# Softmax rows transposed by 32x32 squares on VectorE and through DRAM, with the next image's convolution placed inside attention

## What is computed

```
hdn = relu(w1[m] @ perceive(x)[m] + b1)      # 32 models, 9*16 shifted channels -> 64
x   = x + w2[m] @ hdn + b2                   # 64 -> 16 channels of each model
theta, phi, g = (W_t x + b_t), (W_p x + b_p), (W_g x + b_g)     # 512 -> 128
attn = softmax(theta^T phi)                  # 1024 x 1024 per image
out  = batchnorm(W_w (attn g) + b_w) + x     # 128 -> 512
```

## Time and profile before

| | before |
|---|---|
| median of 3 runs | 1656.85 us |
| the profiled execution's own time | 1657.71 us |
| its span, first to last instruction | 1655.7 us |
| TensorE / VectorE / ScalarE / GpSimd busy | 98% / 43% / 47% / 15% |
| mean granted TensorE clock | 0.992 |
| DMA queue q1, share of 16 engines | 42.0%, 210.65 MB |

### The profile page before, as it was taken

How to read it: one execution, slowest core, us unless ns; L and a number is a source line. 1 busy time by engine, 2 the same in 40 slices (tenths; PEclk the granted TensorE clock), 3 DMA queues, 4 the chain that set the end, 5 groups by cost and what they waited for, 6 DMA issues and landing times.

```text
span 1655.7 us, 26446 instructions
## 1 busy us (share of the span) xinstructions
PE 1617.6 (98%) x9476; PEld 952.3 (58%) x9476; DVE 706.1 (43%) x1200; ACT 774.1 (47%) x1349; POOL 243.3 (15%) x134
## 2 busy tenths in 40 slices
PE   5899999999999999999999999999999999999998
PEld 1276482845738466483754838457384664837557
DVE  0154262543626345262542625335263452625436
ACT  1444454544455454454544545444554544545444
...
GB/s 283 152 157 52 219 81 98 193 38 250 57 125 159 51 250 51 163 126 83 206 51 229 72 107 182 38 263 51 131 158 40 249 51 186 102 88 200 51 0 51
DMA packets 82238, 210.83 MB, mean 127 GB/s; under 512 B 7728, under 2 KB 42544, under 8 KB 82224
## 3 DMA queue, kind: packets, MB, share of 16 engines
q1 hardware_dynamic: 82224, 210.65, 42.0%
...
...
## 4 chain that ended last, share of the span: by engine, by line
PE 89%; issue 3%; DVE 3%; ACT 2%; DMA 2%; SPq 1%; DVEq 0%; ACTq 0%
PE ps L326 27%; PE ps L337 8%; PE ps L348 7%; PE ps L391 6%; PE ps L357 5%; PE ps L359 5%; PE ps L358 5%; PE ps L401 4%; PE ps L402 4%; PE ps L403 4%; PE ps L374 3%; PE ps L375 3%; PE ps L373 3%; PE ps L414 2%; PE ps L415 2%
## 5 line engine op out<-in xcount | busy, mean ns | idle before, releaser
L326 PE MATMUL ps<-windows,w_main 128*64 128x512 f32 x2048 | 489.8, 607 | 16.3 <-DMA windows<-in_x 14.6
L513 ACT ACTIVATE hidden<-ps,columns 128x512 f32<-128x512 f32 x512 | 310.2, 689 | 407.4 <-PE ps L337 407.4
L326 PEld LDWEIGHTS ps<-windows,w_main 128*64 128x64 f32 x2048 | 133.7, 137 | 313.2 <-issue 253.4
L746 POOL TENSOR_TENSOR probs<-probs,row_inv 128x1024 f32<-128x1024 f32 x64 | 121.3, 1895 | 1274.6 <-DVE row_inv L640 1274.6
L622 DVE TENSOR_TENSOR x_lo<-x,x_hi 128x512 fp32r<-128x512 f32 x128 | 88.7, 693 | 372.8 <-ACT x_hi L520 372.8
L549 ACT CAST x_lo<-ps 128x512 fp32r<-128x512 f32 x256 | 139.3, 590 | 120.3 <-PE ps L391 115.4
L634 DVE TENSOR_REDUCE neg_max<-ps 128x1 f32<-128x1024 f32 x128 | 155.9, 1218 | 86.8 <-PE ps L375 85.7
L651 DVE TENSOR_TENSOR x_lo<-ps,x_lo 128x512 fp32r<-128x512 f32 x256 | 164.3, 683 | 33.8 <-ACT x_lo L549 33.8
L357 PE MATMUL ps<-x_hi,wp_hi 128*128 128x512 f32 x384 | 156.2, 407 | 7.1 <-DVE x_lo L622 5.4
L614 DVE SCALAR_TENSOR_TENSOR x<-ps,columns,windows 128x512 f32<-128x512 f32 x128 | 96.0, 750 | 147.8 <-PE ps L348 147.8
L401 PE MATMUL ps<-x_lo,arena 128*128 128x256 f32 x512 | 149.5, 292 | 2.3 <-DVE x_lo L651 1.2
...
## 6 DMA issues: line engine op xcount, KB each, us to landing
windows<-in_x SPq DMA_DIRECT2D x208, 562.0 KB, 13.0
...
```

The costliest lines, as they stand in the source:

```text
L326: mm(ps[rows, hidden_bank(s, q), :], w_main[:, p, which, :], shifted(windows[:, w, :], unit // UNITS, half), start=True, stop=False, skip_ ...
L513: activation(hidden[:, q, :], ps[:, hidden_bank(s, q), :], ACT.Relu, bias=b1s[:, column:column + 1]).then_inc(hidden_ready, 1)
L746: nc.gpsimd.tensor_tensor(rows, rows, row_inv[:, e].to_broadcast([P, PIXELS]), ALU.mult).then_inc(normalized, 1)
```

## The change

1. TensorE's 72 transposes are gone, and with them `round_transposed` and `split_transposed`. VectorE transposes each normalized block in place by 32x32 squares (`transpose_row`), SyncE writes it to a DRAM buffer (`send_row`, 512 KB) and reads it back with the squares' places exchanged (`fetch_row`, in runs of 1 KB), ScalarE rounds it (`round_row`, 1024 elements at once) and GpSimd subtracts (`split_row`). `g` goes the same way, with `split_g` on VectorE.
2. `probs` holds 3 blocks and not 4; `exp_rows` of block i waits until block i-3 has been written to DRAM. `hidden` is no longer used for softmax rows.
3. Slots 0 to 5 of the next image's convolution lie between the steps of attention, with 5 PSUM banks for the hidden layer and not 6. All engines' orders are new. The fetched rows lie in `x1_hi` and `x1_lo`, whose layout is by halves.
4. The waits for the stores stand in `sum_x1` of slots 0 and 4. The store of quarter 3 is issued behind the window loads of groups 0 and 1.

The diff, cut to its core (`send_g`, `fetch_g`, `transpose_g`, `split_g`, `round_g` are as their row counterparts; `mains`, `outputs`, `add_outs` and `relus` loop over the functions of before):

```diff
+BLOCK = 32
 BN_EPS = 1e-5
...
 x1 = sb("x1", [P, BLOCKS, PIXELS])
-x1_hi = sb("x1_hi", [P, BLOCKS, PIXELS], F32R)
-x1_lo = sb("x1_lo", [P, BLOCKS, PIXELS], F32R)
+x1_hi = sb("x1_hi", [P, 2, BLOCKS, HALF], F32R)
+x1_lo = sb("x1_lo", [P, 2, BLOCKS, HALF], F32R)
...
-probs = sb("probs", [P, 2, PIXELS])
+probs = sb("probs", [P, ROWS_HELD, PIXELS])
...
+rows_out = nc.dram_tensor("rows_out", (QBLOCKS + 1, P, PIXELS), F32).ap()
+def squares(row):
+    return row.rearrange("p (a k c) -> p a k c", a=4, c=BLOCK)
+def pt_raw(i):
+    return x1_lo[:, i // 2 % 2, :, :].rearrange("p k n -> p (k n)")[:, i % 2 * PIXELS:(i % 2 + 1) * PIXELS]
+def pt_hi(j):
+    return x1_hi[:, j % 2, :, :].rearrange("p k n -> p (k n)").rearrange("p (m c) -> p m c", m=QBLOCKS)
+def pt_hi_squares(i):
+    return pt_hi(i // 2)[:, :, i % 2 * P:(i % 2 + 1) * P].rearrange("p k (a c) -> p a k c", a=4)
+def pt_lo(j, m):
+    return x1_lo[:, j % 2, :, :].rearrange("p k n -> p (k n)").rearrange(
+        "p (a k c) -> p k a c", a=8, c=BLOCK)[:, m, :, :]
...
+g_raw, g_t = hidden_halves[:, 0, :], hidden_halves[:, 1, :]
...
+HIDDEN_BANKS, BANK_Y, BANK_DX = 5, 6, 5
+FIRST_SLOT_BANKS = [4, 5, 7, 6]
...
+PROJECTIONS = [(0, TH, 2), (0, PH, 6), (1, PH, 7), (0, G, 4), (1, G, 6), (1, TH, 7)]
...
+    def row_back(i):
+        return rows_out[i].rearrange("(a r) (b n) -> (r b) a n", a=4, b=4)
+    def send_row(n, i):
+        sp.wait_ge(transposed, n * QBLOCKS + i + 1)
+        sp.dma_start(rows_out[i], probs[:, i % ROWS_HELD, :]).then_inc(row_sent[i], 16)
+    def fetch_row(n, i):
+        sp.wait_ge(row_sent[i], (n + 1) * 16)
+        sp.dma_start(pt_raw(i).bitcast(F32).rearrange("p (a n) -> p a n", a=4), row_back(i)
...
     def batch(n, has_next, has_second):
         if has_next:
             load_freed(n + 1, GROUPS - 1)
-        for j in range(QUARTERS):
-            store_quarter(n, j)
+        send_row(n, 0)
+        send_g(n)
+        fetch_row(n, 0)
+        send_row(n, 1)
+        fetch_g(n)
+        fetch_row(n, 1)
+        for i in range(2, 5):
+            send_row(n, i)
+            fetch_row(n, i)
+        send_row(n, 5)
+        store_quarter(n, 0)
+        fetch_row(n, 5)
+        send_row(n, 6)
+        store_quarter(n, 1)
+        fetch_row(n, 6)
+        send_row(n, 7)
+        fetch_row(n, 7)
+        store_quarter(n, 2)
         if has_second:
-            for grp in range(GROUPS - 1):
-                load_freed(n + 2, grp)
+            load_freed(n + 2, 0)
+            load_freed(n + 2, 1)
+        store_quarter(n, 3)
+        if has_second:
+            load_freed(n + 2, 2)
...
+        if i == GROUP_PAIRS or i >= 2 * HIDDEN_BANKS - 1:
+            pe.wait_ge(hidden_ready, n * SLOT_PAIRS + max(i - HIDDEN_BANKS, 0) + 1)
+        elif isinstance(n, int) and n == 0:
+            return
+        elif s > 0:
+            pe.wait_ge(exp_done, (n - 1) * QBLOCKS + QBLOCKS - (1 if hidden_bank(s, q) < 2 else 0))
+        elif q == 0:
+            pe.wait_ge(proj_biased, (n - 1) * 6 + proj_step(0, G) + 1)
+        elif q == 1:
+            pe.wait_ge(x1_ready, n * SLOTS)
+        elif q == 2:
+            pe.wait_ge(tp_split, n * 4)
...
+    def attend(n, j, has_next):
         if j > 0:
             pe.wait_ge(out_added, n * 8 + 2 * j - 1)
+        else:
+            pe.wait_ge(g_split, n + 1)
+            if has_next:
+                pe.wait_ge(hidden_ready, (n + 1) * SLOT_PAIRS + GROUP_PAIRS)
+        pe.wait_ge(pt_split, n * QBLOCKS + 2 * j + 2)
         bank = ps[:, y_bank(j), 0:QUARTER]
         for m in range(QBLOCKS):
+            mm(bank, g_hi[:, m, :], pt_hi(j)[:, m, :], start=(m == 0), stop=False)
+            mm(bank, g_lo[:, m, :], pt_hi(j)[:, m, :], start=False, stop=False)
+            last = mm(bank.rearrange("p (a c) -> p a c", c=BLOCK), g_hi[:, m, :], pt_lo(j, m),
+                      start=False, stop=(m == QBLOCKS - 1))
         last.then_inc(y_summed, 1)
...
+        every = range(GROUP_PAIRS)
+        project(n, 0, TH)
         dx(n, SLOTS - 1)
+        project(n, 0, PH)
+        project(n, 1, PH)
+        project(n, 0, G)
         scores(n, 0)
         scores(n, 1)
+        project(n, 1, G)
+        scores(n, 2)
+        project(n, 1, TH)
+        scores(n, 3)
+        scores(n, 4)
+        if has_next:
+            mains(n + 1, 0, every)
             hidden_shared(n + 1, 0)
+        scores(n, 5)
+        if has_next:
+            mains(n + 1, 1, range(0, 1))
+        scores(n, 6)
+        attend(n, 0, has_next)
+        if has_next:
+            dx(n + 1, 0)
+            mains(n + 1, 1, range(1, 3))
+        outputs(n, 0)
+        scores(n, 7)
+        attend(n, 1, has_next)
+        if has_next:
+            mains(n + 1, 1, range(3, 4))
+            hidden_shared(n + 1, 1)
+        outputs(n, 1)
+        if has_next:
+            mains(n + 1, 2, every)
+            hidden_shared(n + 1, 2)
+        attend(n, 2, has_next)
+        if has_next:
+            dx(n + 1, 1)
+            mains(n + 1, 3, every)
+        outputs(n, 2)
+        if has_next:
+            dx(n + 1, 2)
+            hidden_shared(n + 1, 3)
+            image_slot(n + 1, 4)
+            mains(n + 1, 5, every)
+            hidden_shared(n + 1, 5)
+        attend(n, 3, has_next)
+        if has_next:
+            dx(n + 1, 4)
+        outputs(n, 3)
+        if has_next:
+            image_slot(n + 1, 6)
+            image_slot(n + 1, 7)
...
+        if q == 0 and s > 0:
+            act.wait_ge(dx_summed, n * SLOTS + s)
+        elif q == 0 and not (isinstance(n, int) and n == 0):
+            act.wait_ge(g_split, n)
...
+    def round_row(n, i):
+        act.wait_ge(row_landed[i], (n + 1) * 16)
+        nc.scalar.copy(pt_hi_squares(i), squares(pt_raw(i).bitcast(F32))).then_inc(pt_rounded, 1)
...
         bias_projection(n, 0, TH)
+        round_x1(n, SLOTS - 1)
         bias_projection(n, 0, PH)
         bias_projection(n, 1, PH)
         bias_projection(n, 0, G)
         exp_rows(n, 0)
         exp_rows(n, 1)
+        bias_projection(n, 1, G)
         bias_projection(n, 1, TH)
+        exp_rows(n, 2)
+        exp_rows(n, 3)
+        round_row(n, 0)
+        round_g(n)
+        exp_rows(n, 4)
+        if has_next:
+            relus(n + 1, 0, range(0, 2))
+        round_row(n, 1)
+        if has_next:
+            relus(n + 1, 0, range(2, 4))
+        exp_rows(n, 5)
+        round_row(n, 2)
+        exp_rows(n, 6)
+        round_y(n, 0)
+        round_row(n, 3)
+        exp_rows(n, 7)
+        round_y(n, 1)
+        round_row(n, 4)
+        if has_next:
+            relus(n + 1, 1, every)
+        round_row(n, 5)
+        round_y(n, 2)
+        if has_next:
+            round_x1(n + 1, 0)
+            relus(n + 1, 2, range(0, 3))
+        round_row(n, 6)
+        if has_next:
+            relus(n + 1, 2, range(3, 4))
+            round_x1(n + 1, 1)
+            relus(n + 1, 3, range(0, 2))
+        round_row(n, 7)
+        if has_next:
+            relus(n + 1, 3, range(2, 4))
+            round_x1(n + 1, 2)
+            relus(n + 1, 4, every)
+            round_x1(n + 1, 3)
+        round_y(n, 3)
+        if has_next:
+            for s in range(5, SLOTS):
+                relus(n + 1, s, every)
+                round_x1(n + 1, s - 1)
...
+        if grp == 0 and not (isinstance(n, int) and n == 0):
+            dve.wait_ge(stored[half], n * 32)
...
+    def transpose_row(n, i):
+        dve.wait_ge(normalized, n * QBLOCKS + i + 1)
+        if i == 0:
+            dve.wait_ge(projected, n * 6 + proj_step(0, G) + 1)
+        elif i == 2:
+            dve.wait_ge(projected, n * 6 + proj_step(1, TH) + 1)
+        elif i % 2 == 0:
+            dve.wait_ge(y_summed, n * QUARTERS + i // 2 - 1)
+        row = probs[:, i % ROWS_HELD, :]
+        nc.vector.transpose(row, row).then_inc(transposed, 1)
...
+        sum_x1(n, SLOTS - 1)
         split_projection(n, 0, TH)
+        split_x1(n, SLOTS - 1)
         split_projection(n, 0, PH)
         split_projection(n, 1, PH)
         find_max(n, 0)
+        find_max(n, 1)
         invert_sum(n, 0)
         invert_sum(n, 1)
+        transpose_row(n, 0)
+        transpose_g(n)
+        find_max(n, 2)
+        transpose_row(n, 1)
         split_projection(n, 1, TH)
+        invert_sum(n, 2)
+        find_max(n, 3)
+        find_max(n, 4)
+        transpose_row(n, 2)
+        invert_sum(n, 3)
+        split_g(n)
+        invert_sum(n, 4)
+        transpose_row(n, 3)
+        find_max(n, 5)
+        find_max(n, 6)
+        invert_sum(n, 5)
+        transpose_row(n, 4)
+        split_y(n, 0)
+        invert_sum(n, 6)
+        transpose_row(n, 5)
+        add_out(n, 0, 0)
+        find_max(n, 7)
+        add_out(n, 0, 1)
+        invert_sum(n, 7)
+        split_y(n, 1)
+        transpose_row(n, 6)
+        add_outs(n, 1)
+        transpose_row(n, 7)
+        if has_next:
+            sum_x1(n + 1, 0)
+        split_y(n, 2)
+        if has_next:
+            split_x1(n + 1, 0)
+            sum_x1(n + 1, 1)
+        if has_next:
```

(25 more changed lines are left out.)

247 lines of the change are left out of this document (67 added, 180 removed).

## The result

The changed kernel takes 1752.24 us (median of four runs, 1749.71 to 1761.43), the one before 1656.82 beside it: ratio 1.0596, 95% interval 1.055 to 1.0641. It is slower, and far outside the range of the prediction. The profiled execution has a span of 1750.2 us against 1655.7.

What follows compares the result with a forecast made beforehand. TensorE bounds the kernel: a 91.4 us floor plus waits of 1.3, 2.3 and 3.7 gives a 98.7 us period against 100.45, 26 us less over 15 periods; the last image adds 10, making 1641 us, range 1580 to 1698.

Steps and rivals of the forecast that it cites:

- The floor: TensorE's work per image without the transposes' 7.9 us: 91.4 us a period.
- Wait 1: TensorE before scores(4), for VectorE's split of the last projection behind find_max and transposes: 1.3 us an image.
- Wait 2: TensorE before attend(0), for GpSimd's normalizes and subtractions of rows 0 and 1: 2.3 us an image.
- Wait 3: TensorE before dx of slot 5, for slot 4's sum_x1 behind the landed store of quarter 3: 3.7 us, 1.4 to 4.6.
- Rival B: TensorE's clock falls to half behind the dx wait, if that nears 4.4 us: 1688 us; chance 0.14.
- rival D: GpSimd and VectorE block each other, split_g delaying split(0) and attend(0) by 0.9 us: 1655 us, no change; chance 0.06.
- Rival C: Row trips cost 4.4 us a leg (1698 us), or a VectorE transpose costs 2.4 (1711 us); chance 0.10.
- The last image: Row trips are bare without convolution between steps: 72.4 us for 62.1 before, so 10 us more.
- The sum: Floor and three waits make a 98.7 us period against 100.45; with the last image, 1641 us; forecast's chance 0.42.

Runs made afterwards that it cites:

- e10: Changed kernel with three of group 1's five windows loaded behind quarter 3's store, row subtraction on VectorE, last image's rounding, subtraction and fetches reordered; 1657.8 us.
- e2: Changed kernel with twenty unused 512-column matmuls on TensorE between the mains of slot 6 and dx of slot 5; 1727.2 us.
- e3: Changed kernel with the rows' low parts subtracted on VectorE instead of GpSimd; 1728.3 us.
- e9: Changed kernel without the sends and fetches of rows and g through DRAM, output not the reference's attention; 1745.4 us.
- e12: Kernel e10 with four of group 3's nine windows issued one at a time between the rows' fetches; 1770.4 us.

## Why the prediction was wrong

**The floor, right but for 2 us.** The transposes' 7.9 us are gone. e10, at full clock and with its waits known, shows 93.4 us of TensorE an image for my 91.4. Before, the same prices fell short by less: 100.0 busy for 91.4 + 7.9, so 0.7. The other 1.3 is not settled; weight loads that wait for relu grew from 36.5 us over the whole run before to 148.6 in the changed kernel, with five hidden banks for six, and no run isolates that.

**Wait 1, scores(4):** 1.3 predicted, 0.67 measured. **Wait 2, attend(0):** 2.3 predicted, 1.39 measured, with GpSimd's subtraction named as I had it. That it is shorter is no merit of the walk. GpSimd was ready 38.2 us into the image for the walked 36.2: its two subtractions cost 1.0 more than priced, and it stood for 1.6 in between. TensorE came still later, at 37.0 for 34.0, of which the relu wait is 2.4.

**Wait 3, dx of slot 5: the place right, the size wrong, and this decided.** Its walk holds to 0.1 us up to the issue: the store goes out 2.45 us before slot 6's mains end, as walked (85.0 and 87.4). What failed is the sentence "at 0.34 MB/us they are through at 87.4; the store lands at 90.3". The movers, busy throughout from 806 to 814, gave 225 GB/s behind the store's issue and 286 ahead of it, 3.4 MB in 13.3 us or 0.26 MB/us. The store landed 6.7 us after issue for 5.3, and the wait is 5.12 for 3.7, past my high end of 4.6, for which I had taken 0.30. The stretch of the earlier trace rows that I took as a low rate for loads was none for loads with a store behind them. The sums were also off by themselves: 2.9 MB at 0.34 MB/us from 78.1 end at 86.6 and not at 87.4, which makes the wait 2.9, and the high end comes to 4.1 and not 4.6. With that slip put right the forecast would have been further off.

**Rival B came with it.** I had written that it decides "from a wait near those 4.4 us" and gave it 0.14, although my own high end lay beyond. Its price was right: 2.6 predicted, about 2.4 from the busy time (95.72 against e10's 93.4), 1.8 recovered in e2, where the clock fell in other places. With the wait, it makes 1.4 + 2.4 = 3.8 us an image, 57 us.

**The relu wait was not on the list.** I walked `split_g` at 1.25 us and never asked who waits for it; rival D asked what GpSimd loses, not what VectorE does. `split_g` is the one that is blocked, at 2.64 us, and the first relu of slot 0, whose bank slot 1 needs, hangs on it: 2.44 us an image, 37 in all. It was a term put at nothing. e3 shows 1.2 of the 2.44 to be GpSimd's subtraction beside it. In e9 `split_g` is kept out as long (2.86 us) but starts 2.5 us earlier, as g makes no trip, and there is no relu wait: g's late landing is the other half. The rule of the Trainium skill (SBUF — State Buffer, "Who interferes with whom"), that of VectorE and GpSimd the one that starts second blocks fully, agrees with the trace: `split_g` started 0.75 us behind GpSimd's subtraction and ended 1.1 behind it, its own 1.3 us after the port came free at about 753.2 to 753.4. GpSimd's own time stayed at 2.38. In e9 the order is turned: there `split_g` started first, and GpSimd's subtraction took 3.38.

**Rival C, dear trips, gave little in this kernel:** without them the period is 0.1 us shorter (e9), though a send lands in 5.0 us and a fetch in 4.3 in the median, together over the 2 x 4.4 from which I had it decide. They lie for the most part beside GpSimd's chain, and the 1.1 us of waiting that they do cost came back as lower clock when they went. e12, at about 7 us a row, shows the mechanism.

**The last image:** 82.6 for 72.4 walked. Its trips cost 2.8 us (e9), the GpSimd subtraction 3.2 (e3). From 1690 on TensorE is idle for 45% of the time, and what runs is at a lower clock (busy time by stretch, columns as above: the last image of the kernel before, then that of the changed kernel):

```profile
1593.64:1655.70 62.06, 55.68 (x348) 47.41 (x344) 34.26 (x61) 28.10 (x50) 15.16 (x8) 0.99 0.10 34
```

```profile
1667.62:1750.20 82.58, 55.71 (x276) 45.91 (x272) 36.18 (x53) 27.84 (x41) 33.71 (x16) 0.90 0.41 140
```

My walk ran at full clock throughout. TensorE is as long at work as in the last image before, though 72 transposes are gone: by their 7.9 us an estimate of some 8 us for the lower clock. How much of it lies on the path, and how the 10 us divide, was not tried.

**The sum.** 91.4 + 2.0 (floor) + 9.9 (five waits) + 2.4 (clock) = 105.7 us, the measured period. My 98.7 had 7.3 of waits. The 7.0 between them are 2.4 of relu wait, 2.4 of clock, 2.0 of floor, 1.4 at dx and 0.2 before attend(1), less 1.5 at the waits 1 and 2. The failure of method was to treat as alternatives three things that come together: B, D and the forecast's own wait.

**What wasn't tried:** a buffer of its own for g, of 4 KB a partition, which would free the relus from `split_g`.
